# Seven 256-column block products in place of eight for context x query-key and context x value-output, in a two-stage cross attention kernel

## The reference

```
# layer 1: softmax attention of x (256 rows) over the context (256 rows)
q = x @ w_q.T ; k = ctx @ w_k.T ; v = ctx @ w_v.T
probs = softmax(q @ k.T / sqrt(512))
x1 = x + alpha * (probs @ v) @ w_o.T
# layer 2: channels are the 256 rows, positions the 512 columns; no softmax
g_x = g_w @ ctx + g_b ; theta = theta_w @ x1 + theta_b ; phi = phi_w @ ctx + phi_b
y = (theta.T @ phi / 512) @ g_x.T
out = batchnorm(w_w @ y.T + w_b) + x1
```

## Time and profile before

| | us |
|---|---|
| time, median of 3 runs | 388.72 (388.38 to 389.26) |
| profiled execution: span from first to last instruction | 386.3 |
| PE busy | 381.0 (99%) |
| DVE busy | 310.8 (80%) |
| ACT busy | 205.4 (53%) |
| POOL busy | 3.7 (1%) |

### The profile page before, as it was taken

The page is one execution under the profiler, slowest core; times in us unless marked ns, Lnnn a source line. Parts: engine busy times, 40 slices in busy tenths (PEclk is TensorE's granted clock), DMA queues, the critical chain, the costliest instruction groups (busy, mean ns, idle before and its releaser), DMA issues.

```text
span 386.3 us, 5597 instructions
## 1 busy us (share of the span) xinstructions
PE 381.0 (99%) x1776; PEld 318.6 (82%) x1776; DVE 310.8 (80%) x595; ACT 205.4 (53%) x441; POOL 3.7 (1%) x7
## 2 busy tenths in 40 slices
PE   8999999999999999999999999999999999999995
PEld 5888878888888888888888888888888888888885
DVE  4999779987599776996689866996779875996786
ACT  3477568533664267543665257452665346552553
POOL 0001000000000000000000000000000000000000
PEclk9999999999999999999999999999999999999999
DMA  8995842486375646556383556565375564043423
GB/s 242 382 331 188 285 133 54 158 296 225 116 256 145 238 141 211 182 171 217 109 271 112 214 170 198 189 198 188 123 219 181 191 190 136 15 121 144 151 87 110
DMA packets 58059, 70.37 MB, mean 182 GB/s; under 512 B 5056, under 2 KB 47936, under 8 KB 54976
## 3 DMA queue, kind: packets, MB, share of 16 engines
q1 hardware_dynamic: 56144, 67.21, 53.2%
q10 hardware_dynamic: 1904, 3.02, 2.5%
HBM read 51.32 MB, written 18.89 MB: 182 GB/s over the span
## 4 chain that ended last, share of the span: by engine, by line
PE 97%; DMA 1%; DVE 1%; ACT 0%; issue 0%; SPq 0%
PE bank L367 23%; PE bank L368 23%; PE bank L369 23%; PE bank L421 8%; PE bank L440 7%; PE bank L407 5%; PE bank L429 4%; PE bank L462 2%; PE bank L466 1%; DMA xb<-w_k 1%; DVE xb L1143 0%; DVE xb L1138 0%; PE bank L393 0%; ACT theta_hi L621 0%; ACT t_sides L621 0%
## 5 line engine op out<-in xcount | busy, mean ns | idle before, releaser
L367 PE MATMUL bank<-ov_hi,c_sides 128*128 128x512 f32 x128 | 50.0, 391 | 0.0
L368 PE MATMUL bank<-c_sides,qk_hi 128*128 128x512 f32 x128 | 49.9, 390 | 0.0
L369 PE MATMUL bank<-c_sides,qk_lo 128*128 128x512 f32 x128 | 49.9, 390 | 0.0
L368 PE MATMUL bank<-ov_lo,c_sides 128*128 128x512 f32 x128 | 49.9, 390 | 0.0
L367 PE MATMUL bank<-c_sides,qk_hi 128*128 128x512 f32 x128 | 49.8, 389 | 0.0
L369 PE MATMUL bank<-ov_hi,c_sides 128*128 128x512 f32 x128 | 49.8, 389 | 0.0
L621 ACT ACTIVATE t_sides<-bank 128x512 fp32r<-128x512 f32 x32 | 19.0, 594 | 37.2 <-PE bank L369 37.2
L421 PE MATMUL bank<-t_sides,xT_hi 128*128 128x512 f32 x128 | 31.9, 391 | 0.0
L877 DVE TENSOR_TENSOR vo_lo<-bank,vo_hi 128x512 fp32r<-128x512 f32 x32 | 21.8, 685 | 11.8 <-ACT vo_hi L621 10.9
L621 ACT ACTIVATE probs<-bank 128x512 f32<-128x512 f32 x16 | 9.4, 585 | 37.9 <-PE bank L429 37.9
L367 PEld LDWEIGHTS bank<-ov_hi,c_sides 128*128 128x128 f32 x128 | 24.1, 188 | 5.2 <-DVE wg_sides L877 0.4
(11 more groups left out here) (148 smaller groups left out, 820.9 us busy)
## 6 DMA issues: line engine op xcount, KB each, us to landing
cT_raw<-ctx_t SPq DMA_DIRECT2D x8, 1024.0 KB, 4.8
xT_raw<-x_t SPq DMA_DIRECT2D x8, 1024.0 KB, 5.1
c_raw<-ctx_n SPq DMA_DIRECT2D x8, 1024.0 KB, 6.5
xb<-x SPq DMA_DIRECT2D x16, 512.0 KB, 4.2
out<-xb SPq DMA_DIRECT2D x14, 512.0 KB, 2.8
gram_moved<-gram_blocks SPq DMA_DIRECT2D x16, 256.0 KB, 2.3
gram_blocks<-gram_moved SPq DMA_DIRECT2D x64, 64.0 KB, 2.0
moved<-blocks SPq DMA_DIRECT2D x16, 256.0 KB, 2.3
```

Of the source, the lines that this page charges most:

```text
L367: pe.matmul(dst, ahi, bhi, start=(k == 0), stop=False)
L368: pe.matmul(dst, ahi, blo, start=False, stop=False)
L369: mm = pe.matmul(dst, alo, bhi, start=False, stop=(k == k_tiles - 1))
```

## The change

The two context products become the Strassen-Winograd form: the 512x512 factors (qk or ov, and the contexts of a pair side by side, 512 rows by 2 x 256 columns) are cut into 2x2 blocks of 256x256, and seven block products M1 to M7 of 256-column matmuls take the place of eight (`half_product`, 12 matmuls each).

The sums of blocks that the seven products need are new. Of the weights they are made once at the start by DVE (`weight_blocks`, seven scalar_tensor_tensor operations for qk and seven for ov instead of four low parts each); their high parts are ACT's, the low parts DVE's for qk (four) and POOL's for ov. Of the context they are made for each pair on POOL (`mixes`: four sums, then four low parts), with four high parts on ACT between. POOL also takes the low parts of phi_w and theta_w.

The products are summed in the banks as a chain: M1, then M6, M7 and M4 are added into one bank; after M1 ACT copies that bank to another one, into which M2 is added (`copy_chain`); ACT copies M5 to SBUF (`keep_join`); DVE adds chain and kept M5 back into M5's bank (`join`), into which M3 is added, and later chain and side into the side (`join_side`). PE waits for copy, join and side join (`tT_copied`, `tT_joined`, `vo_copied`, `vo_joined`).

Storage moves with it: x1 takes the place of vo, theta that of pT, and the context mixes that of the context rows, so the next context is loaded only after the mixes (`mix_lo`). At the start wo's high parts move from DVE to ACT, and the t tiles' low parts all stand ahead of the normalisation chain on DVE. Scores wait for all of tT at once.

```diff
+PRODUCTS = 7
+M1, M2, M3, M4, M5, M6, M7 = range(PRODUCTS)
+A11, A12, S4, A22, S1, N2, S3 = range(PRODUCTS)
+T1, N2C, T3, N4C = range(4)
+MIXED_SIDE = {M4: N4C, M5: T1, M6: N2C, M7: T3}
...
-            def t_tile(m):
-
-                product(bank[TT_BANK[m]][:].rearrange("p (b s) -> p b s", b=2), lambda k: cut(qk, every, k, tile(m)),
-                        lambda k: cut(cT, every, k),
-                        KH).then_inc(tT_done, 1)
+            def context(i, kt):
+
+                if i in MIXED_SIDE:
+                    return cut(mix, every, MIXED_SIDE[i], kt)
+                k, b = {M1: (kt, 0), M2: (2 + kt, 0), M3: (2 + kt, 1)}[i]
+                return cut(cT, every, k, b)
+
+            def half_product(dst, lhsT, rhs, opens):
+
+                for n in range(2):
+                    for kt in range(2):
+                        (ahi, alo), (bhi, blo) = lhsT(n, kt), rhs(n, kt)
+                        at = dst[:, n * S:(n + 1) * S]
+                        pe.matmul(at, ahi, bhi, start=(opens and n == 0 and kt == 0), stop=False, skip_group_check=True)
+                        pe.matmul(at, ahi, blo, start=False, stop=False, skip_group_check=True)
+                        mm = pe.matmul(at, alo, bhi, start=False, stop=(kt == 1), skip_group_check=True)
+                return mm
+
+            def t_product(i, to_bank, opens=False):
+
+                half_product(bank[to_bank], lambda n, kt: cut(qk, every, i, kt, tile(n)),
+                             lambda n, kt: context(i, kt), opens).then_inc(tT_done, 1)
+
+            def v_product(i, to_bank, opens=False):
+
+                half_product(bank[to_bank], lambda n, kt: [t[:, tile(n)] for t in context(i, kt)],
+                             lambda n, kt: cut(ov, every, i, kt), opens).then_inc(vo_done, 1)
...
-            pe.wait_ge(qk_lo, KH)
+            pe.wait_ge(qk_lo, 1)
+            pe.wait_ge(qk_summed, 4)
             pe.wait_ge(cT_lo, 2)
-            both_rows(0)
-            t_tile(0)
-            pe.wait_ge(ov_lo, 2)
-            both_rows(1)
-            pe.wait_ge(ov_lo, KH)
-            t_tile(1)
+            t_product(M1, TT_CHAIN, opens=True)
+            pe.wait_ge(qk_sum_lo, 1)
+            pe.wait_ge(mix_lo, 1)
+            t_product(M5, TT_JOIN, opens=True)
+            pe.wait_ge(tT_copied, 1)
+            pe.wait_ge(qk_sum_lo, 2)
+            pe.wait_ge(mix_lo, 2)
+            t_product(M6, TT_CHAIN)
+            pe.wait_ge(qk_lo, 3)
+            t_product(M2, FIRST_TT_SEED)
+            gram_rows(0, 0, FIRST_GRAM_BANK)
+            pe.wait_ge(tT_joined, 1)
+            pe.wait_ge(qk_sum_lo, 3)
+            pe.wait_ge(mix_lo, 3)
+            t_product(M7, TT_CHAIN)
+            pe.wait_ge(ov_lo, 3)
+            pe.wait_ge(ov_summed, 4)
+            gram_rows(0, 1, FIRST_GRAM_BANK)
+            for i in range(KS):
+                gram_rows(1, i, FIRST_GRAM_BANK)
+            pe.wait_ge(qk_sum_lo, 4)
+            t_product(M3, TT_JOIN)
+            pe.wait_ge(tT_joined, 2)
+            pe.wait_ge(mix_lo, 4)
+            t_product(M4, TT_CHAIN)
+            pe.wait_ge(wg_factor_lo, 2)
             pe.wait_ge(gram_read, 1)
-            t_tile(2)
-            pe.wait_ge(gram_read, 2)
-            t_tile(3)
-            pe.wait_ge(wg_factor_lo, 2)
-            pe.wait_ge(tT_lo, 2)
             combine_w_g()
...
+                v_product(M1, VO_CHAIN, opens=True)
+                if not first:
                     pe.wait_ge(phi_turned, p + 1)
-                for st in range(KS):
-                    values(0, st)
+                v_product(M5, VO_JOIN, opens=True)
+                pe.wait_ge(vo_copied, two[1])
+                v_product(M6, VO_CHAIN)
+                v_product(M2, VO_SEED)
+                pe.wait_ge(vo_joined, two[1])
+                v_product(M7, VO_CHAIN)
                 if first:
                     pe.wait_ge(phi_turned, p + 1)
                 else:
@@ -546,9 +606,10 @@
                         w_g_phi([0], LAST_T1_BANK[0])
                     else:
                         w_g_phi([0, 1], T1_BANK)
-                for st in range(KS):
-                    values(1, st)
-                pe.wait_ge(vo_lo, four[2])
+                pe.wait_ge(vo_joined, two[2])
+                v_product(M4, VO_CHAIN)
+                v_product(M3, VO_JOIN)
+                pe.wait_ge(vo_lo, four[3])
...
+                pe.wait_ge(x1_made, four[2])
+                t_product(M1, TT_CHAIN, opens=True)
+                pe.wait_ge(mix_lo, four[5])
+                t_product(M5, TT_JOIN, opens=True)
+                pe.wait_ge(x1_made, four[4])
                 theta_rows(0, [four[1], four[2]])
-                pe.wait_ge(x1_made, four[4])
-                t_tile(1)
+                pe.wait_ge(tT_copied, two[3])
+                pe.wait_ge(mix_lo, four[6])
+                t_product(M6, TT_CHAIN)
+                t_product(M2, TT_SEED)
+                pe.wait_ge(gram_read, two[3])
                 theta_rows(1, [four[3], four[4]])
+                pe.wait_ge(tT_joined, two[3])
+                pe.wait_ge(mix_lo, four[7])
+                t_product(M7, TT_CHAIN)
                 pe.wait_ge(gram_read, two[4])
-                t_tile(2)
                 pe.wait_ge(t1_lo, two[1])
                 pe.wait_ge(theta_lo, two[1])
                 for ct in range(KL):
                     output(0, ct)
-                t_tile(3)
-                pe.wait_ge(tT_lo, four[5])
+                pe.wait_ge(tT_joined, two[4])
+                pe.wait_ge(mix_lo, four[8])
+                t_product(M4, TT_CHAIN)
+                t_product(M3, TT_JOIN)
+                pe.wait_ge(theta_lo, two[2])
                 pe.wait_ge(gram_lo, two[4])
                 phi_gram(PHI_BANK)
                 pe.wait_ge(t1_lo, two[2])
-                pe.wait_ge(theta_lo, two[2])
-                pe.wait_ge(tT_lo, four[6])
...
+                copy_chain(VO_SEED, VO_CHAIN, vo_done, seven[1], vo_copied)
                 exp(1)
-                vo_part(0, 0)
+                keep_join(vo_side, VO_JOIN, vo_done, seven[2], vo_copied)
+                if not last:
+                    c_sums(loads[32], batches=[0])
+                vo_part(0, HALF[0], VO_SEED, seven[4])
+                pT_part(0)
+                if not last:
+                    c_sums(loads[32], batches=[1])
+                vo_side_part()
+                if last:
+                    t1_part(0)
+                vo_part(0, HALF[1], VO_CHAIN, seven[6])
                 if first:
                     xT_part(0, loads[32])
-                vo_part(0, 1)
-                if first:
-                    xT_part(1, loads[32])
-                pT_part(0)
+                vo_part(1, HALF[0], VO_JOIN, seven[7])
+                pT_part(1)
...
+                mix_part(T3, four[7])
+                act.wait_ge(x1_made, four[3])
+                copy_chain(TT_SEED, TT_CHAIN, tT_done, seven[8], tT_copied)
+                mix_part(N4C, four[8])
+                keep_join(tT_side, TT_JOIN, tT_done, seven[9], tT_copied)
                 theta_part(0)
-                if not first:
-                    xT_part(0, loads[32])
-                tT_part(1, four[6])
+                xT_part(1 if first else 0, loads[32])
+                tT_part(UPPER, 0, TT_SEED, seven[11])
+                theta_part(1)
                 if not first:
                     xT_part(1, loads[32])
-                theta_part(1)
                 if not first:
                     act.wait_ge(v_made, two[2])
                     fetch_sums(stores[32 * BLOCKS])
@@ -860,8 +982,9 @@
                 if first:
                     act.wait_ge(v_made, 2)
                     fetch_sums(stores[32 * BLOCKS])
-                tT_part(2, four[7])
-                tT_part(3, four[8])
+                tT_side_part(two[4])
+                tT_part(LOWER, 0, TT_CHAIN, seven[13])
+                tT_part(UPPER, 1, TT_JOIN, seven[14])
...
+            def join(side, join_bank, chain_bank, done, count, kept, copied, joined):
+                dve.wait_ge(copied, kept)
+                dve.wait_ge(done, count)
+                dve.tensor_tensor(bank[join_bank][:], bank[chain_bank][:], side.rearrange("p n s -> p (n s)"),
+                                  ALU.add).then_inc(joined, 1)
+
+            def join_side(side, chain_bank, done, count, joined):
+                dve.wait_ge(done, count)
+                dve.tensor_tensor(side, in_halves(chain_bank), side, ALU.add).then_inc(joined, 1)
+
+            def tT_part(rows, b, src, count):
+                dve.wait_ge(tT_hi, count)
+                dve.tensor_tensor(t_sides[:, rows, b, 1], src, t_sides[:, rows, b, 0].bitcast(F32),
+                                  ALU.subtract).then_inc(tT_lo, 1)
...
+                join(vo_side, VO_JOIN, VO_CHAIN, vo_done, seven[3], two[2], vo_copied, vo_joined)
+                vo_part(0, HALF[0], in_halves(VO_SEED), four[1])
```

(70 more changed lines are left out.)

384 lines of the change are left out of this document (213 added, 171 removed).

## The result

The change makes the kernel slower: 447.81 us median (446.77 to 448.33, four runs) against 388.55 (388.04 to 389.26) on the same chip, a ratio of 1.1515 with a 95% interval of 1.1494 to 1.1537. The prediction was 426.5 with a range to 447: the sign was right, and the time lies 0.8 above the range's end. The profiled execution has a span of 445.5, which is 59.2 over the span of before.

The account below looks back on a forecast made before the run. TensorE was taken as the bound, busy 381.0 of 386.3 us. Span 386.3 + start 19.2 + clock 1.4 + first pair 2.3 + six pairs 13.8 + last 1.2 = 424.2, plus 2.4 to the median: 426.5, range 395 to 447.

Parts of the forecast that it names:

- Columns: Context products on TensorE: fewer columns save 1.8 us a pair, 14.4 in all; a pair without waits lasts 42.4.
- The start: Before the first scores: GpSimd's mixes behind its all-reduce, then VectorE's queue, bring the scores at 61.0 against 41.84, 19.2 late.
- M5 starts at 31.7 + 8.0 + 0.2: In the start: all-reduce ends at 31.7, five GpSimd operations at 1.6 and a handover follow, so M5 starts at 39.9.
- the end of the chain: Start, behind VectorE's queue: DMA issues, a high part and handovers 2.1, then combining w and g 0.7, to scores at 61.0.
- VectorE's work alone, 9.5: Start with GpSimd out of the way: VectorE's added operations and ScalarE's 2.1 alone make the scores 9.5 us late.
- The first pair gets the same: First pair: same lengthening as a steady pair, 2.3 us, its own waits for u, t1 and joins summing alike.
- the term for the clock: TensorE after the start's idle time runs at a lower clock: 1.4 us once, bounds 0 and 2.8.
- A pair: Steady pair, scores to scores: TensorE's waits for VectorE and ScalarE make it 46.5 against 44.24 us, 13.8 over six pairs.
- delta: Value-output phase: delta of the first batch waits for the third value block's low part, 2.2 us of stall a pair.
- The fourth: Rival: GpSimd and VectorE block each other, making the side 1.1 later in each value-output phase; 434 us, chance 0.10.
- GpSimd as the bound: Rival: GpSimd's operations take 3.2, start 8 later and M5 waits 2.6 for mixes seven times; 453 us, chance 0.12.
- the second rival: Rival: only the start is lost, VectorE catches up and pairs take 42.4; 395 us, chance 0.12.

Follow-up runs that it names:

- run 12: Changed kernel with GpSimd's mixes ahead of the all-reduce, side join and value side's high part earlier, all mixes on 32 of 512 columns: 417.8 us.
- Run 1: Changed kernel with GpSimd's start context sums and all low parts ahead of the all-reduce, nothing else changed: 436.0 us.
- run 9: Changed kernel with GpSimd's mixes ahead of the all-reduce and the start's mixes alone on 32 of 512 columns: 435.2 us.
- run 14: Changed kernel, mixes before all-reduce on 32 columns, side join and side high part earlier, normalisation chain moved into VectorE's gaps around the start's joins: 416.2 us.
- Run 2: Changed kernel with GpSimd's mixes in the pairs on 32 of 512 columns, same instructions and waits: 435.2 us.
- runs 3 and 4: Each on the changed kernel: VectorE's query-key side join before second xT and theta low parts, 448.4 us; ScalarE's value-side high part before second batch's context sums, 447.6.
- 5: Changed kernel with the pairs' mixes on 32 of 512 columns, plus query-key side join and value side's high part earlier: 431.6 us.
- run 11: Changed kernel with pairs' mixes on 32 columns, side join and side high part earlier, theta low part and gram closing before second xT low part: 456.2 us.
- run 10: Changed kernel, mixes before all-reduce, side join and side high part earlier, GpSimd's mixes of pairs 2 to 7 held until the context's low parts: 447.3 us.

## Why the prediction was right and where it was wrong

**Columns: right.** A pair without waits was put at 42.4; run 12 gives 42.8.

**The start: the term was mis-sized, 19.2 forecast, 26.9 found.** Three of its steps failed. "M5 starts at 31.7 + 8.0 + 0.2": the price of an addition (1.6) was too high, 1.25, but the additions begin at 37.08, not 31.7, since the all-reduce costs a second stretch of idle time behind it; together M5 comes 3.6 later than forecast. The trace of before had the first such stretch, 9.74, and no operation behind it on which a second could show. Then M5 to the side join took 9.7, not 7.5, at the lower clock; the stretch of VectorE's queue behind it was right (11.1 against 10.8); and the end of the chain took 4.3 instead of 2.8. Run 1 shows the queue (7.9 at the scores), 9 the shutting out (5.9 more). What the forecast had for VectorE's work alone, 9.5, is 13.2 in run 9 and 7.8 in run 14: 5 to 6 of it is order, though what a better order wins at the scores is mostly lost again. Whether the last 7.8 is order or load no run shows.

**The first pair: the step that failed most for its size.** "The first pair gets the same" gave 2.3, carried over from the steady pair and not worked out from the first pair's own rows; it is 8.8. Run 2 shows 5.4 of it to be GpSimd's hold on VectorE. The rest fits the first scores at the lower clock, the ten products alone 1.5 (the term for the clock had 1.4 in all).

**A pair: the mechanism only half.** 46.5 was forecast and 47.84 found, 47.3 to 47.7 in the last four of the six. The waits came where the timelines put them: ahead of the fourth product (1.5 forecast, 1.0 on average), the next scores (0.3, 0.24) and delta (2.2, about 1.8), with one more of 0.5 for the first join. But they were put down to order, and runs 3 and 4 show that order alone is worth nothing while GpSimd runs: in the steady pair VectorE is idle for 0.6 us in all from 236.5 to 259, and a wait that is taken away turns up at the next thing it makes. Runs 2 and 5 give the split: 0.7 for GpSimd, 0.9 more for the orders. Of the 21.6 that six pairs lost, 9.6 are left in run 12.

**The rivals.** The fourth, by which POOL and DVE block each other, was real; it had 0.10, and was priced at one wait of 1.1 in a pair, 7.7 in all. Without GpSimd's work in the pairs the kernel gains 12.6 (run 2; by the pieces 5.4 in the first pair and 5.8 in the six), and without its mixes in the start 5.9 at the scores (run 9). It is not an alternative to the forecast but a term of it. GpSimd as the bound did not come: apart from its first, PE waits for no mix. Nor did the second rival: no run has a pair near 42.4. The last pair lost 1.9 instead of 1.2.

Left open is how much of an earlier start could be kept: run 14 shows the loads in the first pair's way, but no run moved them. Left open too is the wait of 1.15 a pair ahead of phi that remains in run 12, since run 11, which was to take it away, ran into the loads.

## What to carry to other kernels

Work that is moved to GpSimd isn't off VectorE if both then read SBUF: look at which of VectorE's operations in that stretch have two SBUF inputs, and compare with just doing the work on VectorE (here 449.7 against 447.8). Where an engine is full over a stretch, take a wait's worth from what that engine makes next, not from the wait; and count, for an operation that is moved back, the buffer that it releases, since the load that waits for it may land on a short transfer that is on the path.

## What was not expected of the hardware

- Between the all-reduce and the next addition POOL idles for 7.36 us with nothing to wait for, besides the 7.51 ahead of the all-reduce; with the all-reduce last, only 5.59 ahead of it remain.
- GpSimd's additions of 128x512 take 1.25 us in the start, where VectorE is idle, and up to 2.34 in a pair, beside VectorE's low parts of the context; the hold seems to go both ways.
- Behind waits of 1.72 us (kernel after), 1.86 (run 9) and 2.15 (run 10) PE's granted clock fell towards 1.2 GHz, and 512-column products were 0.43 us apart instead of 0.23. Behind others as long, 1.90 in the kernel after and 2.15 in another pair of run 10, it did not.
